# Expert weights of a routed feed-forward layer: prepared on TensorE and ScalarE beside and behind the first layer norm

## What is computed

```python
x = x + 0.5 * ffn(layernorm(x), Wr, Wup, bup, Wdn, bdn)   # x: 4096 x 256, fp32
x = x + attention(layernorm(x), ...)
x = x + 0.5 * ffn(layernorm(x), Wr, Wup, bup, Wdn, bdn)

def ffn(x):                                # 8 experts, 2 per token
    top, idx = top_k(x @ Wr, 2);  w = scatter(softmax(top), idx)
    gu = x @ Wup[e] + bup[e]               # Wup[e]: 256 x 512
    gate, up = min(gu[::2], 7), clip(gu[1::2], -7, 7)
    act = (up + 1) * gate * sigmoid(1.702 * gate)
    return sum_e w_e * (act @ Wdn[e] + bdn[e])          # Wdn[e]: 256 x 256
```

## Time and profile before

| | us |
|---|---|
| median of 3 runs | 808.35 (804.83 to 818.48) |
| span of the profiled execution, first to last instruction | 799.3 |
| last product of the logits ends | 56.9 |
| last one-hot product ends | 82.4 |
| first gather is issued | 83.7 |
| first product with an expert's weights | 90.2 |

### The profile page before, as it was taken

The page is one execution under the profiler, slowest core; times in us unless marked ns, Lnnn a source line. Parts: engine busy times, 40 slices in busy tenths (PEclk is TensorE's granted clock), DMA queues, the critical chain, the costliest instruction groups (busy, mean ns, idle before and its releaser), DMA issues.

```text
span 799.3 us, 13210 instructions
## 1 busy us (share of the span) xinstructions
PE 631.0 (79%) x3712; PEld 527.1 (66%) x3713; DVE 446.0 (56%) x1116; ACT 314.2 (39%) x696; POOL 353.5 (44%) x379
## 2 busy tenths in 40 slices
PE   2673898888878879969998996679898898888900
PEld 2452777776757668858887994568777786767700
DVE  6868653444434436277775986845353444445446
ACT  2663243434333335346663443334243334333400
POOL 2781646565656553513331000155656565656400
PEclk9985999999999998999999999599988999999955
DMA  9871232222222221245542431132212222222179
GB/s 307 295 229 28 73 99 81 70 78 69 85 72 78 78 73 52 93 135 157 157 142 94 150 116 66 8 87 67 79 62 85 70 82 69 79 72 79 54 261 369
DMA packets 52601, 87.99 MB, mean 110 GB/s; under 512 B 16228, under 2 KB 32019, under 8 KB 52054
## 3 DMA queue, kind: packets, MB, share of 16 engines
q1 hardware_dynamic: 17568, 39.52, 15.0%
q0 software_dynamic: 13664, 35.42, 14.3%
q10 hardware_dynamic: 21334, 12.61, 5.1%
HBM read 53.94 MB, written 35.39 MB: 112 GB/s over the span
## 4 chain that ended last, share of the span: by engine, by line
PE 61%; DVE 13%; another core or an unknown queue 8%; DMA 7%; issue 5%; ACT 4%; POOL 0%; SPq 0%; ACTq 0%; DVEq 0%; POOLq 0%
PE ps L854 15%; PE ps L852 13%; PE ps L853 12%; PE ps L843 9%; PE ps L1070 3%; DMA work<-y_dram 3%; PE ps L847 3%; DVE aT_lo L1447 2%; PE ps L877 2%; ACT aT_hi L689 2%; DVE xs L1503 1%; DMA raw_c<-L_ffn_down_proj 1%; PE ps L926 1%; PE ps L869 1%
## 5 line engine op out<-in xcount | busy, mean ns | idle before, releaser
L521 POOL DMA_INDIRECT y_dram<-work,sidx x142 | 142.7, 1005 | 166.7 <-ACT work L706 128.7
L513 POOL DMA_INDIRECT work<-xn_dram,gidx x142 | 140.2, 988 | 47.2 <-issue 43.6
L1455 DVE TENSOR_SCALAR work<-ps 128x256 f32<-128x256 f32 x142 | 57.1, 418 | 147.3 <-issue 83.3
L843 PE MATMUL ps<-cst,work 128*128 128x128 f32 x688 | 109.4, 284 | 29.9 <-DVE aT_lo L1447 22.5
L852 PE MATMUL ps<-up_hi,xT_hi 128*128 x284 | 120.9, 426 | 13.5 <-issue 11.2
L854 PE MATMUL ps<-up_hi,xT_lo 128*128 x284 | 114.1, 402 | 8.6 <-issue 8.2
L853 PE MATMUL ps<-up_lo,xT_hi 128*128 x284 | 113.8, 401 | 8.5 <-issue 7.8
L696 ACT ACTIVATE work<-ps 128x256 f32<-128x256 f32 x142 | 52.1, 393 | 171.7 <-PE ps L854 129.8
L843 PEld LDWEIGHTS ps<-cst,work 128*128 128x128 f32 x688 | 84.3, 145 | 52.3 <-issue 35.3
L852 PE MATMUL ps<-dn_hi,aT_hi 128*128 x284 | 96.7, 340 | 0.0
L706 ACT ACTIVATE work<-ps,slot_gate 128x256 f32<-128x256 f32 x142 | 59.5, 471 | 72.2 <-PE ps L854 54.7
(11 more groups left out here) (172 smaller groups left out, 1136.5 us busy)
## 6 DMA issues: line engine op xcount, KB each, us to landing
work<-y_dram SPq DMA_DIRECT2D x32, 512.0 KB, 4.3
xn_dram<-work ACTq DMA_DIRECT2D x29, 255.0 KB, 2.6
xs<-L_attn_x SPq DMA_DIRECT2D x4, 1024.0 KB, 10.5
work<-q_dram SPq DMA_DIRECT2D x16, 256.0 KB, 2.8
out<-xs SPq DMA_DIRECT2D x16, 256.0 KB, 5.9
q_dram<-work ACTq DMA_DIRECT2D x15, 256.0 KB, 2.3
work<-xn_dram,gidx POOLq DMA_INDIRECT x142
y_dram<-work,sidx POOLq DMA_INDIRECT x142
```

The lines of the kernel that those rows point to most:

```text
L513: pool.indirect_dma_start(xg[:, k, u, 1:H + 1], None, xn_dram[n], bass.IndirectOffsetOnAxis(ap=gidx[:, 2 * s + u:2 * s + u + 1], axis=0)). ...
L521: pool.indirect_dma_start(y_dram[n], bass.IndirectOffsetOnAxis(ap=sidx[:, 2 * s + u:2 * s + u + 1], axis=0), ysb[:, k, u, :], None, bounds ...
L843: ins = nc.tensor.transpose(ps[:, bank, k:k + P], src[:, u, c * P:(c + 1) * P], ident)
L1455: return v.tensor_scalar(upv[:, u, :], ps[:, 2 + 2 * b + u, :].rearrange("p (f c) -> p f c", c=2)[:, :, 1], 1.0 - LIMIT, 1.0 + LIMIT, ALU. ...
```

## The change

Raw weights are loaded straight into the tiles that will hold the low halves (`raw_up`, `raw_dn` are views of `up_w[1]`, `dn_w[1]`), two DMAs for each expert. The order of SP's stream: all four x spans, twelve small loads (six of biases, six of rows), weights 0 and 1, then the sixteen stores of normalised rows (which leave ACT's stream), with weights 2, 3 and 4 behind stores 5, 9 and 12, and weights 5 to 7 behind the last. Eight row buffers take the place of five. POOL makes a matrix `fold` (identity with a first row of -1), `minus` (negative identity) and the split rows. PE folds into PSUM, ACT takes the high half out of PSUM, PE subtracts it, ACT takes the remainder into the low tile; POOL is left with the low half of the down part. Expert 0 is done beside pairs 9 and 10, experts 1 to 3 between the logits and the count, expert 4 behind the count, experts 5 to 7 behind the one-hot products, where the 50 transposes were (layer 1 keeps them). DVE's folds, `last_low` and the first row loads are gone.

```diff
-WEIGHTS_AT = {2: 0, 4: 1, 6: 2, 8: 3, 10: 4, 12: 5}
-RAW = 3
-RAW_OF = [0, 1, 2, 0, 1, 2, 0, 2]
-ROW_OF = [0, 1, 2, 0, 1, 2, 0, 1]
-LAST = E - 1
-ROWS = 5
+TURN_AT = {9: 0}
+BEFORE_GATES, BEFORE_HOTS = 4, 5
+ROWS = 8
+STORES = 4
...
+        def weight_banks(e):
+            at = ((2, 5) if e < len(TURN_AT) else (0, 6))[(e - len(TURN_AT)) % 2] if len(TURN_AT) else (0, 6)[e % 2]
+            return ps[:, at:at + 2, :]
...
+            def load_weights(e):
+                wait(sp, w_loaded[e % 4], 32 * (e // 4))
+                sp.dma_start(raw_up[:, :, e, :], Wup[e].rearrange("(c p) f -> p c f", p=P)).then_inc(w_loaded[e % 4], 16)
+                sp.dma_start(raw_dn[:, :, e, :], Wdn[e].rearrange("(c p) f -> p c f", p=P)).then_inc(w_loaded[e % 4], 16)
+            def store_xn(g):
+                wait(sp, L[0].xn_stored[g % STORES], 16 * (g // STORES))
+                sp.wait_ge(L[0].xn, g + 1)
+                sp.wait_ge(xn_odd, g + 1)
+                sp.dma_start(pair(xn_v[0], g)[:, :, 0:H - 1], xn_f[g % ROWS][:, :, 1:H]
+                             ).then_inc(L[0].xn_stored[g % STORES], 16)
+            for c in range(4):
+                load_x(c)
+            sp.wait_ge(pool_step, 3)
+            for q in (0, Q32, Q64):
+                sp.dma_start(bstage[q:q + E, :], bdn).then_inc(bias_loaded, 16)
+                sp.dma_start(bstage[q + E:q + E + 1, :], bo.rearrange("(a o) -> a o", a=1)).then_inc(bias_loaded, 16)
+                sp.dma_start(rows_f[q:q + E, :], Wup[:, 0, :]).then_inc(rows_loaded, 16)
+                sp.dma_start(rows_f[q + E:q + 2 * E, :], bup).then_inc(rows_loaded, 16)
+            load_weights(0)
+            load_weights(1)
+            for g in range(NG):
+                store_xn(g)
+                if g in (5, 9, 12):
+                    load_weights({5: 2, 9: 3, 12: 4}[g])
+            for e in range(5, E):
+                load_weights(e)
...
+            def make_folds():
+                st.mark(nc.gpsimd.tensor_scalar(minus[:, :], ident, -1.0, None, ALU.mult))
+                st.done(nc.gpsimd.tensor_copy(fold[:, :], ident))
+                st.done(nc.gpsimd.memset(fold[0:1, :], -1.0))
+                st.mark(nc.gpsimd.memset(fold[0:1, 0:1], 0.0))
...
+                pool.wait_ge(rows_loaded, 16 * 6)
+                st.done(nc.gpsimd.tensor_scalar(rows_f, rows_f, sign_of, None, ALU.mult))
+                odd = rows_f.rearrange("p (f c) -> p f c", c=2)[:, :, 1]
+                st.done(nc.gpsimd.tensor_scalar(odd, odd, one, None, ALU.add))
+                st.done(nc.gpsimd.tensor_copy(fold_rows_w[:, :], rows_f))
+                st.done(nc.gpsimd.tensor_tensor(rows_f, rows_f, fold_rows_w[:, :], ALU.subtract))
+                for q in (Q32, Q64):
+                    st.done(nc.gpsimd.tensor_copy(fold_rows_w[q:q + 32, :], rows_f[q:q + 32]))
+                st.done(nc.gpsimd.tensor_tensor(rows_f[Q64:Q64 + 32], rows_f[Q64:Q64 + 32], fold_rows_w[Q64:Q64 + 32, :],
+                                                ALU.subtract))
+                nc.gpsimd.tensor_copy(fold_rows_w[Q64:Q64 + 32, :], rows_f[Q64:Q64 + 32]).then_inc(rows_split, 1)
...
-            for e in range(LAST):
-                pool.wait_ge(up_hi, KC * (e + 1))
-                low(up_w[1][:, :, e, :], raws[RAW_OF[e]][:, 0:KC * F].rearrange("p (c f) -> p c f", c=KC), up_w[0][:, :, e, :])
-                pool.wait_ge(raw_hi, e + 1)
-                low(dn_w[1][:, :, e, :], raws[RAW_OF[e]][:, KC * F:KC * (F + H)].rearrange("p (c f) -> p c f", c=KC),
-                    dn_w[0][:, :, e, :]).then_inc(raw_lo, 1)
+            for e in range(E):
+                pool.wait_ge(dn_hi, e + 1)
+                low(dn_w[1][:, :, e, :], raw_dn[:, :, e, :], dn_w[0][:, :, e, :]).then_inc(dn_lo, 1)
...
-            def high_up(e, c):
-                act.wait_ge(folded, e + 1)
-                nc.scalar.activation(up_w[0][:, c, e, :], raws[RAW_OF[e]][:, c * F:(c + 1) * F], ACT.Copy).then_inc(up_hi, 1)
-            def high_down(e):
-                nc.scalar.activation(dn_w[0][:, :, e, :],
-                                     raws[RAW_OF[e]][:, KC * F:KC * (F + H)].rearrange("p (c f) -> p c f", c=KC),
-                                     ACT.Copy).then_inc(raw_hi, 1)
-            def high_parts(e):
-                for c in range(KC):
-                    high_up(e, c)
-                high_down(e)
+            def up_high(e):
+                act.wait_ge(up_folded, e + 1)
+                nc.scalar.activation(up_w[0][:, :, e, :], weight_banks(e), ACT.Copy).then_inc(up_hi, 1)
+            def up_low(e):
+                act.wait_ge(up_rest, e + 1)
+                nc.scalar.activation(up_w[1][:, :, e, :], weight_banks(e), ACT.Copy).then_inc(up_lo, 1)
+            def down_high(e):
+                act.wait_ge(w_loaded[e % 4], 32 * (e // 4 + 1))
+                nc.scalar.activation(dn_w[0][:, :, e, :], raw_dn[:, :, e, :], ACT.Copy).then_inc(dn_hi, 1)
...
-                if g in WEIGHTS_AT:
-                    high_parts(WEIGHTS_AT[g])
+                if g in TURN_AT:
+                    up_high(TURN_AT[g])
+                    down_high(TURN_AT[g])
+                elif g - 1 in TURN_AT:
+                    up_low(TURN_AT[g - 1])
             logits_out(0)
-            high_parts(LAST - 1)
+            def weights(e):
+                up_high(e)
+                down_high(e)
+                up_low(e)
+            for e in range(len(TURN_AT), BEFORE_GATES):
+                weights(e)
...
+            def up_fold(e):
+                pe.wait_ge(w_loaded[e % 4], 32 * (e // 4 + 1))
+                if e == 0:
+                    pe.wait_ge(consts_made, 2)
+                    pe.wait_ge(rows_split, 1)
+                wait(pe, up_lo, e - 1)
+                banks = weight_banks(e)
+                nc.tensor.matmul(banks[:, 0, :], fold[:, :], raw_up[:, 0, e, :], start=True, stop=False)
+                nc.tensor.matmul(banks[:, 0, :], bias_select[:, e, :], fold_rows_w[:, :], start=False, stop=True)
+                nc.tensor.matmul(banks[:, 1, :], ident, raw_up[:, 1, e, :], start=True, stop=False)
+                nc.tensor.matmul(banks[:, 1, :], select[:, e, :], fold_rows_w[:, :], start=False, stop=True
+                                 ).then_inc(up_folded, 1)
+            def up_remainder(e):
+                pe.wait_ge(up_hi, e + 1)
+                for c in range(KC):
+                    ins = nc.tensor.matmul(weight_banks(e)[:, c, :], minus[:, :], up_w[0][:, c, e, :], start=False,
+                                           stop=True, skip_group_check=True)
+                ins.then_inc(up_rest, 1)
...
+                        up_fold(TURN_AT[g])
+                    elif g - 1 in TURN_AT:
+                        up_remainder(TURN_AT[g - 1])
...
+            def turn_weights(first, last):
+                up_fold(first)
+                for e in range(first, last):
+                    if e + 1 < last:
+                        up_fold(e + 1)
+                    up_remainder(e)
             def route(l):
+                if l is L[0]:
+                    turn_weights(len(TURN_AT), BEFORE_GATES)
...
+                    turn_weights(BEFORE_GATES, BEFORE_HOTS)
...
-                keep_running(50)
+                if l is L[0]:
+                    turn_weights(BEFORE_HOTS, E)
+                    pe.wait_ge(up_lo, E)
+                    pe.wait_ge(dn_lo, E)
+                else:
+                    keep_running(50)
                 pe.wait_ge(l.routed, 1)
-                pe.wait_ge(raw_lo, LAST)
-                pe.wait_ge(raw_hi, LAST)
```

More of the change, by code:

```diff
@@ L61 @@
 Q32, Q64 = 32, 64
+LOGITS = 7
 WORK = 8192
@@ L233, in build @@
         logit_T = area(2688, 2, P)
-        first_rows = [first_row[:, b, :] for b in range(2)] + [area(6208, F)]
-        raws = [area(3136, 1536), area(4672, 1536), raw_c[:, :]]
-        xn_f = [area(at, 2, H) for at in (0, 512, 6720, 7232)] + [rows_c[:, :, :]]
+        xn_f = [area(at, 2, H) for at in (0, 512, 6720, 7232, 3136, 3648, 4160, 4672)]
+        rows_f = area(5184, F)
         qk_raw = area(7168, KC, 2 * H)
@@ L314, in __init__ @@
                 s = self.s
-                self.xn_stored = [s(f"xn_stored_{j}") for j in range(2 if n else ROWS)]
+                self.xn_stored = [s(f"xn_stored_{j}") for j in range(2 if n else STORES)]
                 self.xn_T, self.xn_Tsb = s("xn_T"), s("xn_Tsb")
@@ L402, in load_folded @@
                 sp.dma_start(dst[0:1, 0, :], w_bias.rearrange("(a o) -> a o", a=1)).then_inc(loaded, 16)
-            for e in range(2, E):
-                load_raw(e)
             sp.wait_ge(L[0].x_T, turned(RING))
@@ L658, in gates @@
                 if n == 0:
-                    act.wait_ge(raw_loaded[RAW_OF[LAST]], 96 * RAW_OF.count(RAW_OF[LAST]))
-                    high_down(LAST)
+                    for e in range(BEFORE_GATES, BEFORE_HOTS):
+                        weights(e)
                 for ch in range(NQC):
@@ L752, in _ @@
             gates(0)
```

(40 more changed lines are left out.)

84 lines of the change are left out of this document (32 added, 52 removed).

## The result

The kernel before took 811.5 us (median of 18 runs, 802.8 to 818.5), the changed one 818.0 (18 runs, 810.4 to 822.4): ratio 1.0087, 95% interval 1.0063 to 1.0112, that is 7.1 us (5.1 to 9.1), a small loss and within 2%. The forecast was 813.4 with 802 to 828, out of +5.1 us.

The account below looks back on a forecast made before the run. PE was taken to pace the layer norm, the effect being a shift of the experts' start: -11.7 + 4.3 - 0.6 + 11.65 - 0.35 + 1.8 = +5.1; 799.3 became 804.4, plus 9.05 around the span 813.4, range 802 to 828.

Parts of the forecast that it names:

- Layer norm, -11.7: Start to end of the logits: PE sets the pace, expert 0 adds 6.3; logits end at 45.2 instead of 56.9.
- Count +4.3: Between logits and count: experts 1 to 3 on PE delay the count to 12.15 behind the logits instead of 7.9.
- Expert 4 fits into the 5.5 in which PE waits: Behind the count: expert 4's preparation fits PE's wait for DVE's slots, at worst 1.6 us late at half clock.
- DVE's pace over the eight chunks stays: Between count and last one-hot product: DVE works through its eight chunks as fast as before, no change in time.
- Gather +11.65: Last one-hot product to first gather: POOL's low half of expert 7 holds the gather until 13.0 behind, instead of 1.35.
- Turning to first product -0.35: First tile's turning to first expert product: `last_low` no longer stands before x's low half, saving 0.35 us of 2.07.
- Clock at the start, +1.8: Start of the experts: PE idles 5.2 us before the gather lands, so nine products run at half clock, 1.8 us more.
- What lies around the span: Outside the profiled execution: 9.05 us from its forecast 804.4 to the median, making 813.4.
- Rival A: Weight preparation behind logits and one-hot products: PE at half clock costs 7 + 7.5 us, 828 in all; chance 0.17.
- B: Layer norm's loads: x or rows land late, first span at about 12, giving 816 to 819; chance 0.15.
- C: Layer norm gains more: logits end at 41, no clock loss at the experts' start, 807 (floor 801); chance 0.18.
- D: Before count and gather: weight preparation is not what holds the gather, 4.3 and 11.65 fall away, 797; chance 0.04.

Follow-up runs that it names:

- e4: Changed kernel with one expert less before the count (two before it, two behind): 709.1 us, ratio 1.0058 to the kernel before.
- e0: The changed kernel itself, measured again in another group: 805.56 us, ratio 1.0070 to the kernel before.
- e5: Changed kernel with DVE making the low halves of experts 5 to 7, without PE's remainder, ACT's low copy and POOL's low half: 793.28 us, ratio 0.9924.
- e1: Changed kernel with ACT taking the down parts of experts 5 to 7 ahead of the eight chunks, so POOL's low halves come early: 710.99 us, ratio 1.0076.
- e2: Changed kernel with 50 unneeded transposes behind the last weights, to keep PE at work until the gather lands: 711.16 us, ratio 1.0078.
- e9: The kernel of e5 again (DVE makes the low halves of experts 5 to 7), in a group of 704 us: 707.06 us, ratio 1.0039.
- e6: As e5, but three experts instead of four turned before the count and four in the tail, low halves by DVE: 706.01 us, ratio 1.0030.
- e10: As e5, but no expert beside the layer norm, two before the count, one behind it, five in the tail: 702.19 us, ratio 0.9954.
- e8: As e10, but in layer 0 PE turns the first tiles ahead of the last weights, and six transposes are left out: 698.02 us, ratio 0.9913.

## Why the prediction was right, and where it was off

The sign, the size (+5.1 against 7.1, 5.1 to 9.1) and the place were right: a gain in the layer norm, given back before the count and before the gather. Within the size there is some luck: terms that were wrong cancel, as the list shows.

- **Layer norm, -11.7: measured -12.1**, with errors inside that cancel. The first x span landed 5.2 behind its issue, not 7.1, and DVE began its statistics at 6.5, so the second pair was done at 17.5, not 20.7. (The Trainium skill, "DMA: Bandwidth & Descriptors", "Queues, rings and completion order": descriptors of one ring start in ring order. Four spans in a row did not hold the first one up, which agrees.) Expert 0 took 7.0 instead of 6.3, and 2.2 went in waits at the change of a span, of which 0.52 and 0.57 stand in the first fence: "DVE runs ahead from the start" was too kind.
- **Count +4.3: measured 12.3 behind the logits, forecast 12.15.** e4 confirms that it is the third expert.
- **"Expert 4 fits into the 5.5 in which PE waits": failed.** Its fold ran at half clock and ACT's copies of it stood ahead of L702. Forecast: last one-hot product 17.0 behind the count's start; measured 18.45, so 1.5 too little. The count itself got no full clock either (1.21 instead of 0.75, in that 1.5).
- **"DVE's pace over the eight chunks stays": failed too, in the same place.** The second chunk took 1.06 longer beside POOL's low half of expert 4. In the changed kernel's trace this ends in the same 0.1 us as PE's late first product, so either alone would have held the third chunk back (in e0, where that product is at half clock, DVE waits 0.78 for it). In e5's trace the fold ran at full clock (1.10) and the first one-hot product still came 7.5 behind the count, now waiting for DVE; the last one began 16.9 behind it, against 17.3 in the changed kernel's trace and 16.4 before.
- **Gather +11.65 (13.0 behind the last product): measured 14.2.** The fold of expert 5 ran at half clock (2.00, 1.12). The cause was right, as e1 and e5 show, but it is not the only one: freed of it alone, the stretch from the list to the first tile is 2 us shorter, since the weights are ready only then.
- **Turning to first product -0.35: nothing.** 2.05 (93.24 to 95.29) against 2.07 before.
- **Clock at the start, +1.8: 1.0 at most, and cancelled.** The products did run at 0.43 until 98, and from the first product to the third step it took 1.0 longer than before; the first gather's landing, 1.0 shorter, covered it. In e2, which restored the clock, the third step waited for its gather instead. (The rule in the Trainium skill, "TensorE: Matmul & The Clock Gate", "Why this matters for your kernels", that idle gaps cost the clock, agrees with the rows: PE stood 4.7 us and the granted clock was 0.50 from 90 to 98. That the clock then costs time holds only where PE sets the pace.)
- Together: the first gather was forecast 3.65 later than before (-11.7 + 4.3 - 0.6 + 11.65) and came 6.1 later, by 1.5 + 1.2 + 0.15 less the 0.4 that the layer norm gained more. Without the 1.8 for the clock the sum would have been 3.3; that term, mostly wrong in itself, brought it near by luck.
- **What lies around the span** was taken as 9.05. It is 1.8 here (819.3 for a span of 817.5) and 1.75 to 3.0 in all runs whose span is on record; the profiled execution of before was a quick one among 802.8 to 818.5. The forecast's base was the median of three runs, 808.35, which is 3.2 under the median of 18; so of the 4.6 by which 813.4 missed 818.0, 3.2 are the base and 1.4 the change (5.1 against 6.5 between the medians).

Rival A (half clock while preparing weights) was not true between logits and count (granted clock 1.00), and behind the count and behind the one-hot products only for the first fold of each; it cost at most 2.7 where it would have cost 14.5. (Its 0.77 from the earlier trace rows is from a window in which PE was busy 5.00 of 5, so it wasn't a sign of gaps.) B fell with the first span. C would need logits at 41; D is excluded by e1 and e5: the waits were real.

## What to carry to other kernels

When preparation moves from idle engines to the one that everything queues behind, price each step by the stream it stands in: one expert cost 6.4 to 7 us beside the layer norm, 4 in a row of folds, and 1.8 to 3.5 in the tail where DVE made its low half in one operation (list to first tile: 11.9 with three experts in e9, 15.4 with four in e6, 17.2 with five in e10). Where two conditions hold a start, take away both before judging either. And compare the moment at which the edited part ends with the time: if the rest of the program wanders by more than the edit, that moment is the better measure of what the edit did, though not of the time.

## Not expected

- The same program takes 705 or 800 to 813 us: between single products with an expert's weights PE stands for up to 1.4 us, and no semaphore ends the wait, in some groups of runs, and not at all in others (134 against 160 us busy in 160, clock 0.99 and 1.00).
- A version under the kernel before: e8, 0.9913 (0.9893 to 0.9934), in a group of 704; the changed kernel, over it in both of its groups, was not run in that one. It keeps the change's folds in PSUM and loads, makes no expert beside the norm, and lets DVE make the low halves of the last five.
- DVE's subtraction out of PSUM into fp32r, 1024 columns, takes 1.22, ACT's copy of the same columns 1.02 and the two products before it 0.82; the same chunk operation on DVE took 0.68 alone and 1.21 beside POOL's subtractions.
